# Turning the normalised tokens by DMA instead of on TensorE, in a vision-transformer block of 128 images

## What is computed

```python
h = tok(x)                               # 16x16 patches, real part of rfft2, projection to 192, class token, position
h = h + attn(layernorm(h))               # 12 heads of 16 features, softmax, output projection
h = h + ffn(layernorm(h))                # 12 heads of 64 features, layernorm on q and k, softmax, gated heads, projection
```

## Time and profile before

| | |
|---|---|
| median of three runs | 5536.16 us |
| span of the profiled execution | 5532.4 us |
| TensorE matmul busy | 5344.4 us (97%) |
| VectorE busy | 4923.8 us (89%) |
| ScalarE busy | 4327.1 us (78%) |
| GpSimd busy | 2985.7 us (54%) |
| granted TensorE clock | nine tenths or more of full speed in every slice |
| DMA | 19 GB/s over the span |

### The profile page before, as it was taken

The page is one execution under the profiler, slowest core; times in us unless marked ns, Lnnn a source line. Parts: engine busy times, 40 slices in busy tenths (PEclk is TensorE's granted clock), DMA queues, the critical chain, the costliest instruction groups (busy, mean ns, idle before and its releaser), DMA issues.

```text
span 5532.4 us, 202492 instructions
## 1 busy us (share of the span) xinstructions
PE 5344.4 (97%) x63024; PEld 4563.7 (82%) x63024; DVE 4923.8 (89%) x16193; ACT 4327.1 (78%) x17409; POOL 2985.7 (54%) x3206
## 2 busy tenths in 40 slices
PE   3999999999999999999999999999999999999998
PEld 2788888888888888888888888888888888888887
DVE  5899999999999999999999999999999999999996
ACT  1777887887888788788778878877887887887786
POOL 0555555555555555555555555555555555555554
PEclk9999999999999999999999999999999999999999
DMA  2000000000000000000000000000000000000000
GB/s 72 18 22 18 17 21 17 18 17 21 18 17 21 17 18 17 21 18 17 21 18 17 20 18 18 17 21 18 17 21 17 18 17 21 18 17 21 18 17 6
DMA packets 60519, 106.93 MB, mean 19 GB/s; under 512 B 8076, under 2 KB 33944, under 8 KB 60128
## 3 DMA queue, kind: packets, MB, share of 16 engines
q1 hardware_dynamic: 60456, 106.12, 6.2%
HBM read 86.72 MB, written 19.37 MB: 19 GB/s over the span
## 4 chain that ended last, share of the span: by engine, by line
PE 94%; DVE 4%; issue 1%; ACT 0%; POOL 0%; SPq 0%; DVEq 0%; DMA 0%; POOLq 0%; ACTq 0%
PE bank L491 82%; PE bank L672 10%; PE bank L529 2%; DVE qk L898 1%; DVE qkn L996 1%; SPq L403 0%; ACT p L733 0%; DMA bp<-in_bp 0%; ACT pq L771 0%; POOL pq L475 0%; DVEq L902 0%; DVEq L1025 0%; DVE wqk_mean L804 0%; DVEq L992 0%; DVE nmax L903 0%
## 5 line engine op out<-in xcount | busy, mean ns | idle before, releaser
L475 POOL TENSOR_TENSOR pq<-pq,gn 99x788 f32<-99x788 f32 x768 | 1153.3, 1502 | 914.0 <-DVE gn L1011 913.9
L771 ACT ACTIVATE pq<-bank,nmax 99x197 f32<-99x197 f32 x3072 | 1300.1, 453 | 291.6 <-DVE nmax L1002 291.6
L733 ACT ACTIVATE p<-bank,nmax 99x197 f32<-99x197 f32 x3072 | 1323.1, 467 | 112.0 <-DVE nmax L903 97.3
L484 POOL TENSOR_TENSOR qkb<-qkn,ln_b 128x396 f32<-128x396 f32 x768 | 639.5, 847 | 1164.0 <-DVE qkn L996 1151.4
L777 ACT ACTIVATE pT<-bank 99x394 f32<-99x394 f32 x1536 | 767.6, 518 | 259.4 <-PE bank L672 256.4
L903 DVE TENSOR_REDUCE nmax<-bank 99x2 f32<-99x394 f32 x1536 | 843.2, 563 | 113.9 <-PE bank L491 101.7
L1002 DVE TENSOR_REDUCE nmax<-bank 99x2 f32<-99x394 f32 x1536 | 827.2, 559 | 25.7 <-PE bank L491 10.7
L733 ACT ACTIVATION_READ_ACCUMULATOR p<-bank,nmax 99x1 f32 x3072 | 762.6, 248 | 0.0
L491 PE MATMUL bank<-x2T,wqkc 128*128 128x198 f16 (+1 forms) x7680 | 752.5, 248 | 1.0 <-ACT p L733 0.7
L672 PE MATMUL bank<-ident,pq 99*99 99x99 f32 (+1 forms) x6144 | 725.3, 253 | 7.7 <-ACT pq L771 5.2
L771 ACT ACTIVATION_READ_ACCUMULATOR pq<-bank,nmax 99x1 f32 x3072 | 720.7, 235 | 0.0
(11 more groups left out here) (148 smaller groups left out, 10116.0 us busy)
## 6 DMA issues: line engine op xcount, KB each, us to landing
xa<-in_xa SPq DMA_DIRECT2D x128, 300.1 KB
xb<-in_xb SPq DMA_DIRECT2D x128, 300.1 KB
out_tokens<-res SPq DMA_DIRECT2D x128, 74.2 KB
out_tokens<-res SPq DMA_DIRECT2D x128, 73.5 KB
p<-in_wq SPq DMA_DIRECT2D x1, 1152.0 KB
pT<-in_wk SPq DMA_DIRECT2D x1, 1152.0 KB
qkc<-in_basis SPq DMA_DIRECT2D x1, 661.5 KB
sq<-in_wq SPq DMA_DIRECT2D x1, 576.0 KB
```

The costliest lines, as they stand in the source:

```text
L475: nc.gpsimd.tensor_tensor(pair, pair, factor, op=ALU.mult).then_inc(s_sc.up(), 1)
L484: nc.gpsimd.tensor_tensor(qkb[:, t], qkn[:, t % QKN_SLOTS], ln_b[:].unsqueeze(2).to_broadcast([128, 2, TP]), op=ALU.add).then_inc(s_qk.up( ...
L733: last = nc.scalar.activation(p1[0:TC, h, c, :], psum("s1", h)[0:TC, c * T:c * T + T], ACT.Exp, bias=nmax1[:, c, h:h + 1], accum_out=sum1[ ...
L771: last = nc.scalar.activation(pq[0:TC, h % SLOTS, c, 0:T], psum("s2", h)[0:TC, c * T:c * T + T], ACT.Exp, bias=nmax2[:, h, c:c + 1], accum ...
```

## The change

The four pieces become four runs of 128 columns for each chunk, `parts` and the results get 112 rows instead of 99, and one DMA transpose, issued on SyncE's queue, turns all of `parts` of one layer (112 rows of 1024 float16 values, 229,376 bytes) into `x1T` or `x2T`. The TensorE steps `x1T` and `x2T` and the four copies out of PSUM go. The high and low halves of features 128 to 191 are no longer interleaved, so `normalise` writes the low half with two instructions; ScalarE writes the second high half of features 128 to 191 in new steps `hx1` and `hx2`. The readers wait for the DMA. SyncE's loop becomes a fifth list of `ORDER`; `4:load` in it makes the number of partial rounds ahead of the loop four. All other lists are new as well: the steps stand in another order and in other rounds (for instance `2:ctx2`, `2:wo`, `1:qk0` to `1:qk5`, and `0:s2_2` to `0:s2_10`).

```diff
     "pe": """
+2:ctx2@2 0:s2_2@76 0:s2_4@10 0:rstd5@2 2:wo@4 3:tok@3 0:pT_0@4 1:qk0@7 0:pT_2@5 1:qk1@6 0:pT_1@0 0:pT_3@3 1:qk2@1
+0:s2_6@40 0:s2_8@57 1:ms0@1 1:gl@2 1:qk3@6 1:qk4@3 1:qk5@0 0:pT_5@5 0:pT_4@2 0:pT_6@4 1:ms1 3:qk1_0@2 3:qk1_1@6
+3:qk1_2@3 1:ms2 3:s1_0@20 3:s1_2@64 0:o2_0@7 0:o2_1@5 0:o2_2@3 0:pT_7@7 3:v1@0 3:s1_4@72 0:s2_10@16 0:o2_3@4 1:rstd0@3
+0:pT_8@5 1:v2_0@0 0:pT_9@1 3:s1_6@37 3:s1_8@56 3:ctx0@0 0:o2_4@1 0:pT_11@4 0:pT_10@2 1:v2_2@3 1:rstd1@2 3:s1_10@07
+0:o2_5@4 3:ctx1@5 1:s2_0@61 1:v2_1@2 1:rstd2@4 0:proj@7 1:rstd3@6 1:v2_3@1 1:rstd4@4
     "dve": """
+0:rstd3 0:v2_3 0:rstd4 2:cl2 3:fold 0:s2_2 0:s2_3 0:s2_4 0:s2_5 0:rstd5 0:gr1 2:wo 3:tok 3:nx1 0:s2_6 0:s2_7 0:gr2
+0:s2_8 0:gr3 0:s2_9 1:gl 2:nx2 1:gate1 1:gate2 3:qk1_0 0:gr4 3:qk1_1 3:s1_0 3:s1_1 3:qk1_2 3:s1_2 0:ol0 3:s1_3 1:var2
+0:ol1 3:s1_4 0:ol2 0:s2_10 3:s1_5 0:s2_11 1:rstd0 3:ctx0 1:v2_0 0:gr5 3:s1_6 3:s1_7 0:ol3 3:s1_8 3:s1_9 3:cl0 3:ctx1
+0:ol4 1:rstd1 3:s1_10 3:s1_11 0:ol5 1:gate3 1:s2_0 1:s2_1 1:v2_1 1:rstd2 1:v2_2 3:ctx2 3:cl1 1:gr0 0:proj
     "act": """
+0:s2_1 2:ctx2 0:s2_2 0:s2_3 0:s2_4 0:pT_0 0:s2_5 1:qk0 1:qk1 0:pT_1 0:pT_2 0:pT_3 3:hx1 1:qk2 0:s2_6 0:s2_7 0:s2_8
...
+0:pT_11 3:s1_8 3:s1_9 0:o2_5 3:s1_10 3:s1_11 3:ctx1 1:s2_0 2:hx2
     "pool": """
+0:h2c 0:bias3 0:bias4 1:h2b 0:sc1 0:bias5 2:root2 3:root1 1:sq0 1:sq1 1:sq2 0:sc2 0:sc3 1:sq3 3:h1b 1:sq4 1:sq5 0:sc4
+0:sc5 1:bias0 1:bias1 1:sc0 1:bias2
+    "sp": """
+3:x1T 4:load 0:store 2:x2T
...
-        parts = [sb(f"parts{layer}", [TC, 2, 256, 2], F16) for layer in (1, 2)]
-        x1T = sb("x1T", [128, 4, 2, TC], F16)
+        parts = [sb(f"parts{layer}", [TR, 2, 4, 128], F16) for layer in (1, 2)]
+        x1T = sb("x1T", [128, 2, 4, TR], F16)
...
+            def x1T_(img, _):
+                sp.wait_ge(*s_x1.at(img, 1))
+                sp.wait_ge(*s_xe[0].at(img, 1))
+                if not isinstance(img, int) or img > 0:
+                    sp.wait_ge(*made(img - 1, *last_of("pe", [("v1", 0), *(("qk1", g) for g in range(3))])))
+                sp.sem_inc(s_go[0].up())
+                sp.dma_start_transpose(x1T[:].rearrange("p c k n -> p (c k) n"), parts[0][:].rearrange("p c k x -> p (c k x)")).then_inc(s_xt[0].up(16), 16)
+            def x2T_(img, _):
...
+                    sp.wait_ge(*made(img - 1, *last_of("pe", [("gl", 0), *(("qk", t) for t in range(6)), *(("v2", n) for n in range(4))])))
...
-            def transposes(o, parts):
...
                 if g == 0:
-                    pe.wait_ge(*read_out(img, "x1T", 0))
+                    pe.wait_ge(*s_xt[0].at(img, 16))
...
-            def x1T_(img, _):
-                act.wait_ge(*made(img, "x1T", 0))
-                nc.scalar.activation(x1T[:, 0:2].rearrange("p k c n -> p (k c) n"), turned("x1T")[:, 0:4, 0:TC], ACT.Copy).then_inc(s_xa.up(), 1)
...
+            def x_end(img, layer, x, name):
+                act.wait_ge(*s_step[name].at(img, 1))
+                nc.scalar.activation(parts[layer][0:TC, :, 3, 0:DH], x[:, :, 128:D], ACT.Copy).then_inc(s_xe[layer].up(), 1)
...
+                dve.wait_ge(*s_xt[layer].at(img, 0))
...
-                step(V.tensor_copy(cat[:, :, 0:D, 0], dst[:]), img, name, 2)
-                V.tensor_tensor(cat[:, :, 0:D, 1], dst[:], cat[:, :, 0:D, 0], op=ALU.subtract).then_inc(sig.up(), 1)
+                step(V.tensor_copy(high, dst[:]), img, name, 2)
+                V.tensor_tensor(cat[0:TC, :, 1, DH:128], dst[:, :, 128:D], high[:, :, 128:D], op=ALU.subtract)
+                V.tensor_tensor(cat[0:TC, :, 2, :], dst[:, :, 0:128], high[:, :, 0:128], op=ALU.subtract).then_inc(sig.up(), 1)
...
-            def x1T_(img, _):
-                dve.wait_ge(*s_xa.at(img, 1))
-                V.tensor_copy(x1T[:, 2:4].rearrange("p k c n -> p (k c) n"), turned("x1T")[:, 4:8, 0:TC]).then_inc(free("x1T", 0), 1)
```

## The result

The changed kernel takes 6205.25 us (median of four runs, 6196.77 to 6214.18), the kernel before 5536.41 in the same comparison: 1.121 times as long (95% interval 1.1194 to 1.1226). The forecast was 5452, its range ended at 5600, and 0.30 was given to a slower kernel. It was wrong in sign and far in size.

A forecast was written before the change was run, and what follows sets the result against it. TensorE was taken as the bound: 42.00 us a round less 0.70 transposes and 0.55 wait, plus 0.5 lost, gives 41.25. Over 125 rounds that saves 94 us; 10 added for the ends gives 5452, range 5390 to 5530.

The forecast's parts named there:

- The transposes and copies: TensorE loses 0.70 us of transposes a round; copies leave VectorE and ScalarE, saving VectorE some 0.6 us.
- The DMA: SyncE's transposes of layers one and two: 3.7 us each, hidden by covers of about 5 and 6 us.
- Rival one: DMA transpose slower than its cover, stalling TensorE at `qk1_0` and `qk0`: 0.10 up to the gain, 0.15 beyond.
- Its sum, taken from the store: DMA time from the store's row: 0.76 us to start, 2.1 for 896 rows, 0.8 to the waiting engine; 3.7.
- The estimate of 5.2: DMA time if 56 tiles at 32 sequencer cycles add 1.5 us: 5.2 us, 0.2 over the cover.
- VectorE's new order: `nx1` right behind `tok` on VectorE: its own work becomes 40.15 us a round, below TensorE's 40.75.
- the wait at the root: VectorE stands some 0.8 us a round at `nx1` while GpSimd makes the inverse root.
- What in-order lists lose: Some TensorE waits return because engines run in order: 0.5 us a round, between 0 and 1.1.
- the forecast's 41.25: Predicted round in us: TensorE's 40.75 plus 0.5 lost to in-order lists.
- Rival two: VectorE becomes the bound through `gr0`, `sc0`, `bias2`, `s2_4`: round 42.4 us, 5596 us; chance 0.17, of which 0.13 slower.
- its two signs: TensorE idle over 1.25 us a round at `s2_4` on `qkb`, or VectorE's waits adding up to over 1.85 us.
- Rival three: The new lists lose nothing: round 40.75 us, 5380 us; edge of the forecast's 0.58, no separate chance.

The follow-up runs named there:

- run 12: DMA transposes with the old lists, `hx1` ahead of `s2_0`, several TensorE and VectorE steps moved to fill waits, against the kernel before: 5526.51 us, 0.9982.
- run 5: DMA transposes with the lists of the kernel before, ScalarE's `hx1` ahead of two exponentials, against the kernel before: 5582.9 us, 1.0085.
- run 9: GpSimd's squares, scalings and bias sums cut to 8 columns, in the changed kernel (5548.75 us) and, as control, in the kernel before (5534.72 us).
- run 7: Changed kernel with GpSimd squaring 8 of 198 columns: 5778.98 us, 1.0441 of the kernel before.
- run 3: Changed kernel with ScalarE's `hx1` moved behind `qk2`: 6287.51 us, 1.1355 of the kernel before.
- run 4: As run 3, with GpSimd's `sq0` and `sq1` moved ahead of `root1`: 6281.98 us, 1.1347 of the kernel before.
- run 8: Changed kernel with 20 filler matmuls on TensorE at `ms0`, behind its wait for the bank: 6086.98 us, 1.0999 of the kernel before.

## Why the prediction was wrong

*The transposes and copies: right.* The prediction gave TensorE 40.75 us without them; with the old order it has 40.67 (run 12) to 41.0 (run 5).

*The DMA: right in mechanism, a little dear.* It was taken at 3.7 us within 2.5 to 18 and lands in 2.9. The packets answer the open question of their size: 298,093 against 60,519 before are 928 more for each of the 256 transposes, close to the 896 rows of 256 bytes. Rival one, a DMA later than its cover, did not happen in the changed kernel. Its sum, taken from the store, was 0.8 us too high. The estimate of 5.2 that the prediction drew from the Trainium skill, "DMA: Bandwidth & Descriptors", is not borne out by the 2.9.

*VectorE's new order: the step that failed.* "So its own work is 40.15 us a round. TensorE's 40.75 stays the bound" counted instructions at their old durations and added the wait at the root. That wait was right (0.90 against 0.8). The durations were not: by busy time alone, waits left out, VectorE has 41.4 us, and 4.7 of these go when GpSimd's elementwise work does (run 9). Nothing in the prediction priced what GpSimd does beside VectorE. It could have been seen: in the old lists, GpSimd stood idle beside `nx1` and `nx2`, which is why had 0.66 for the pair; in the new one `sq0` and `sq1` stand right behind `root1`, and the root is what releases `x`. Once their `qkc` are there, the list itself sets the two side by side.

*Why it reaches TensorE.* VectorE stands in a ring with GpSimd, ScalarE and TensorE: `tok`, `root1`, `nx1`, `hx1`, `qk2`'s copy, its bank, `ms0`. The prediction had named the link, "unless `hx1` makes it stand waiting for `nx1`", and gave it nothing; it made ScalarE stand 2.4 us a round, and TensorE 1.94 behind it. With short squares both waits fell by just what `x` became shorter (run 7). Cutting this link (run 3) or moving the squares (run 4) only moved the loss.

*What in-order lists lose: 0.5 was far too little.* By the 20 rounds the changed kernel's TensorE idles (943.00 - 883.76) / 20 = 3.0 us a round, and is busy 44.2 instead of 40.75. At least 1.0 us of the round is the clock (run 8). The prediction took the granted clock of 1.00 as given, though its own rivals made TensorE wait; here the mean was 0.948.

*The new order of TensorE costs by itself.* With GpSimd cut and only 0.28 us idle, TensorE is busy 41.59 in the new order, 0.92 more than the 40.67 of the old order with the same matmuls. A third of it is seen: from the start of the last matmul of an `ms` to the next step the median is 261 ns, against 147 where `ctx` follows it in the old order, three times a round (0.34 us). Where the rest lies was not found. So even without GpSimd beside VectorE the forecast's 41.25 would have been missed, by 0.6.

*Rival two had the right engine for another reason.* VectorE's work did grow past what the round could hide. But the prediction put the place at `gr0`, `sc0`, `bias2` and `s2_4`, and the price at 0.4 us a round; it was 5.2, and TensorE waited for `qkb` once in the whole run, 0.7 us. One of its two signs, waits of VectorE above 1.85 us a round, was met, with 4.4 in the 20 rounds; but it says little, since with GpSimd's work cut they are 3.7 and the loss is gone (run 9). What the sign could not show is the longer instructions, which count as busy. Rival three, lists that lose nothing, had no run near it.

*What stays open.* Runs 7 and 9 cut GpSimd's own time as well as what it does to VectorE. At `nx1` the rows of run 7 part the two, and it is the second; for the whole round they were not parted. That TensorE waited for results of GpSimd itself only 16 us in the changed kernel's whole loop (9.9 for `sq`, 5.2 for `pq`, 0.7 for `qkb`) speaks for the second there too. How the rest of the 5.2 us, less the clock, splits among the links of the ring was not measured. Whether the new lists could be kept with GpSimd's steps set elsewhere was tried only in run 4.

## What to carry to other kernels

Before a new order is priced with old durations, look for each instruction of VectorE between SBUF tiles at what GpSimd does in the same microsecond, before and after: 0.66 us became 1.89 by a neighbour. Where one engine's step releases both VectorE and GpSimd, or GpSimd's result releases VectorE while its next step is ready, they can run side by side in every round. Look for it in the durations: such an instruction shows as longer and busy, not as waiting. A new data path and a new order are worth two measurements: here the path cost nearly nothing with the old order (1.0085, then 0.9982), and the new order took another 11% (6205.25 against 5582.9).

## What the runs showed of the hardware

- Some of VectorE's instructions on SBUF and GpSimd's slow each other: `x` 368 ns alone and 1134 beside GpSimd in the changed kernel, the cast 359 and 631, `fold` 965 before and 1568 after. Which of the two stood longer went by which began first: VectorE's second low half (line 873) began 127 times ahead of a square, and kept 418 ns, while these squares took 951 ns instead of 847. Not all are slowed: the maxima, which read PSUM, kept 0.56 us, and the statistics of 99 x 192 from SBUF took 352 ns beside GpSimd's scaling and 344 alone. The Trainium skill, "SBUF — State Buffer", in the section "SBUF: two separate sides", has this as an exclusive lock on a port pair, held for a whole instruction, in which the other engine blocks; the trace agrees in that the pair of `x` ended one `x` after the squares, and in the 951 ns. The section names VectorE's instructions with two inputs from SBUF, or in a two-port mode; `x` has one tensor from SBUF besides its two columns of scalars, and the trace does not show its mode.
- A DMA transpose of 112 x 1024 float16 values within the chip's memory lands in 2.9 us, its issue holds SyncE's queue for 1.23 us, and in run 5 the 136 `x` beside one took 371 ns in the mean, the others 376.
- After a wait of 1.94 us and the short products of `ms0` and `gl` TensorE's granted clock was 0.57 over 4 us, though not in every round with that wait. With twenty matmuls of 198 columns between the same wait (1.87 us) and `ms0` the clock was 0.993 in the mean and the round 1.0 us shorter.
